# Attention rows and score maxima: other queues and routes for on-chip copies in a fused transformer block

## What is computed

```python
x = x + retention(layernorm(x))     # 4 heads, chunks along the tokens, gated
x = x + channel_mix(layernorm(x))   # sigmoid(xr @ W_r.T) * (relu(xk @ W_k.T)**2 @ W_v.T)
x = x + attention(layernorm(x))     # 16 heads of width 16, softmax with a bias by distance
x = x + channel_mix(layernorm(x))
```

## Time and profile before

| | us |
|---|---|
| median of 3 runs | 3273.11 (3270.3 to 3284.18) |
| the profiled execution | 3270.77 |
| its span, first to last instruction | 3268.8 |
| TensorE busy in it | 3028.9 |
| VectorE, ScalarE, GpSimd busy | 2026.8, 1731.7, 1249.1 |
| mean granted clock of TensorE | 0.949 of 2.4 GHz |

### The profile page before, as it was taken

The page is one execution under the profiler, slowest core; times in us unless marked ns, Lnnn a source line. Parts: engine busy times, 40 slices in busy tenths (PEclk is TensorE's granted clock), DMA queues, the critical chain, the costliest instruction groups (busy, mean ns, idle before and its releaser), DMA issues.

```text
span 3268.8 us, 50303 instructions
## 1 busy us (share of the span) xinstructions
PE 3028.9 (93%) x18786; PEld 1609.8 (49%) x18786; DVE 2026.8 (62%) x3231; ACT 1731.7 (53%) x3667; POOL 1249.1 (38%) x1764
## 2 busy tenths in 40 slices
PE   5969999899998999989999999999999999999998
PEld 3634456444564445644466444664446534465344
DVE  4448735687356863578545785458844588346882
ACT  2417844378343773438734486344754358533674
POOL 2314533245332452325433244333443334433353
PEclk8969999899998999989999899998999989999899
DMA  6060000600006000050001400023000320005100
GB/s 167 1 129 1 2 1 1 142 9 7 1 10 133 15 2 1 30 113 15 2 1 46 97 15 1 1 70 73 14 1 1 98 45 15 1 1 113 30 2 14
DMA packets 54897, 115.87 MB, mean 35 GB/s; under 512 B 10480, under 2 KB 33056, under 8 KB 54528
## 3 DMA queue, kind: packets, MB, share of 16 engines
q1 hardware_dynamic: 54656, 112.67, 15.5%
HBM read 69.24 MB, written 45.11 MB: 35 GB/s over the span
## 4 chain that ended last, share of the span: by engine, by line
PE 79%; DVE 7%; issue 3%; POOL 3%; DMA 3%; ACT 3%; SPq 1%; POOLq 0%; DVEq 0%; ACTq 0%
PE psum L647 18%; PE psum L701 18%; PE psum L523 11%; PE psum L678 9%; PE psum L752 3%; PE psum L546 3%; DMA SQ<-mrow 2%; PE psum L801 2%; PE psum L733 2%; PE psum L787 2%; PE psum L612 2%; PE psum L578 2%; DVE nrm L1238 2%; DVE mx L1358 2%; PE psum L804 2%
## 5 line engine op out<-in xcount | busy, mean ns | idle before, releaser
L1358 DVE TENSOR_REDUCE mx<-psum 128x1 f32<-128x1024 f32 x1024 | 1235.6, 1222 | 249.2 <-PE psum L647 247.1
L1108 ACT ACTIVATE Z<-psum 128x512 f32<-128x512 f32 x2048 | 1114.2, 597 | 411.5 <-PE psum L678 371.5
L1548 POOL TENSOR_TENSOR Z<-Z,band_exp 128x256 f32<-128x256 f32 (+1 forms) x1152 | 713.9, 641 | 932.0 <-ACT Z L1108 924.4
L678 PE MATMUL psum<-SQ,SK 64*128 64x512 f32 x2048 | 884.3, 481 | 39.8 <-DMA SQ<-mrow 39.8
L647 PE MATMUL psum<-SK,SQ 63*128 63x512 f32 x2048 | 798.0, 481 | 47.9 <-DVE mx L1358 27.6
L701 PE MATMUL psum<-Z,Vx 128*17 128x256 f32 x8192 | 643.5, 389 | 0.0
L647 PEld LDWEIGHTS psum<-SK,SQ 63*128 63x128 f32 x2048 | 330.8, 201 | 454.7 <-issue 292.7
L678 PEld LDWEIGHTS psum<-SQ,SK 64*128 64x128 f32 x2048 | 368.3, 189 | 236.7 <-ACT Z L1108 178.6
L523 PE MATMUL psum<-Wqkvg,Z 128*128 128x512 f32 x768 | 380.3, 620 | 18.5 <-ACT Z L1009 18.5
L701 PEld LDWEIGHTS psum<-Z,Vx 128*17 128x17 f32 x8192 | 138.5, 95 | 289.8 <-issue 272.5
L1493 POOL TENSOR_TENSOR Z<-Z 128x512 f32<-128x512 f32 x64 | 81.1, 1268 | 360.0 <-DVE Z L1286 353.9
(11 more groups left out here) (120 smaller groups left out, 3205.4 us busy)
## 6 DMA issues: line engine op xcount, KB each, us to landing
parts<-Z SPq DMA_DIRECT2D x48, 512.0 KB
SQ<-parts SPq DMA_DIRECT2D x48, 256.0 KB, 8.1
SK<-parts SPq DMA_DIRECT2D x48, 256.0 KB, 11.5
X<-L_attn_a_x SPq DMA_DIRECT2D x8, 1024.0 KB, 5.5
parts<-mixed SPq DMA_DIRECT2D x16, 512.0 KB
SQ<-parts SPq DMA_DIRECT2D x16, 512.0 KB, 8.3
SK<-parts SPq DMA_DIRECT2D x16, 512.0 KB, 13.8
out<-X SPq DMA_DIRECT2D x16, 512.0 KB, 8.0
```

The costliest lines, as they stand in the source:

```text
L678: pe.matmul(col_bank(s, i), SK[rows_of(h), h // 2, j * P:j * P + P], SQ[rows_of(h), h // 2, 512 * half:512 * half + 512], start=True, stop ...
L1108: nc.scalar.activation(ring[:, n % RING, :], col_bank(s, i), ACT.Exp)\
L1358: nc.vector.tensor_reduce(mx[:, blk, col:col + 1], bank_pair[u % 2], AX_X, ALU.max)\
L1548: nc.gpsimd.tensor_tensor(ring[:, n % RING, a:z], ring[:, n % RING, a:z], band_exp[:, 4 * hg + COLS[i], at:at + z - a], ALU.mult)\
```

## The change

For heads 0 to 3 the way through memory is replaced: 12 DMAs for q and 12 for k, each of 16 partitions by 1024 numbers, copy from `split[0][s]` to `SQ` or `SK` (`spread_directly`). The stores of heads 0 to 7 shrink to heads 4 to 7, and share 0 is gone. The semaphores are split in the same way: `first_out` (heads 4 to 7), `parts_out` (8 to 15), `spread_first` (the copies). The Relu of q = 2 waits for the copies and `first_out` of q. The maxima of block 0 are sent by ScalarE; SyncE sends those of blocks 1 to 7 and stores batch b−1 before them.

```diff
+        def max_rows_in(eng, blk):
+            h0, q0 = blk // 2 * 4, blk % 2 * 512
+            for hh in range(4):
+                r = HALF * (hh % 2) + MAX_ROW
+                eng.dma_start(SQ_words[r:r + 1, (h0 + hh) // 2, q0:q0 + 512],
+                              mrow[4 * hh:4 * hh + 4, blk % 2, :].bitcast(F32)).then_inc(mx_in[blk % 2].sem, 16)
...
+            def spread_directly(b, s):
+                need(sp, c_lo, b, 3 + s)
+                stack = (SQ_words, SK_words)[s]
+                for h in range(4):
+                    for group, part in enumerate(((1, 0, 0), (0, 1, 0))[s]):
+                        r0 = HALF * (h % 2) + HD * group
+                        sp.dma_start(stack[r0:r0 + HD, h // 2, :],
+                                     split[0][s][HD * h:HD * h + HD, part, :].bitcast(F32))\
+                            .then_inc(spread_first[s].sem, 16)
...
                 need(sp, c_lo, b, 4 * h + 3 + s)
+                p0 = (64, 0)[h]
+                done = (first_out, parts_out)[h][s]
                 for part in range(PARTS):
                     slot = (1 - part, part)[s]
-                    sp.dma_start(parts_scratch[s, 8 * h:8 * h + 8, slot],
-                                 split[h][s][:, part, :].bitcast(F32)).then_inc(parts_out[s].sem, 16)
+                    sp.dma_start(parts_scratch[s, (4, 8)[h]:8 * h + 8, slot],
+                                 split[h][s][p0:P, part, :].bitcast(F32)).then_inc(done.sem, 16)
...
             for b in range(B):
+                for s in range(2):
+                    spread_directly(b, s)
                 for h in range(2):
                     for s in range(2):
                         parts_store(b, h, s)
-                    for share in ((0, 1), (2,))[h]:
-                        for s in range(2):
-                            spread_rows(b, share, s)
-
-                for blk in range(8):
+                    for s in range(2):
+                        spread_rows(b, h + 1, s)
+
+                if b > 0:
+                    store(b - 1)
+                for blk in range(1, 8):
                     need(sp, mx_row, b, blk + 1)
...
                 if q == 2:
-                    need(act, parts_out[0], min(b + 1, B - 1), 2)
+                    need(act, spread_first[0], min(b + 1, B - 1), 12)
+                    need(act, first_out[0], min(b + 1, B - 1), 2)
...
                 max_rows(0)
-
-                for out_side in parts_out:
-                    need(act, out_side, b, 4)
+                need(act, mx_row, b, 1)
+                max_rows_in(act, 0)
+
+                for s in range(2):
+                    need(act, spread_first[s], b, 12)
+                    need(act, first_out[s], b, 2)
+                    need(act, parts_out[s], b, 2)
```

More of the change, by code:

```diff
@@ L265, in build @@
         c_lo = tally("dve", "c_lo", 8)
-        parts_out = [tally("sp", f"parts_out_{side}", 4, 16) for side in "qk"]
-        spread = [tally("sp", f"spread{share}", 8, 16) for share in range(3)]
+        first_out = [tally("sp", f"first_out_{side}", 2, 16) for side in "qk"]
+        parts_out = [tally("sp", f"parts_out_{side}", 2, 16) for side in "qk"]
+        spread_first = [tally("sp", f"spread_first_{side}", 12, 16) for side in "qk"]
+        spread = [None] + [tally("sp", f"spread{share}", 8, 16) for share in (1, 2)]
         p_vx = tally("pe", "p_vx", 4)
@@ L419, in _ @@
                 .then_inc(s_band, 16)
+            def spread_directly(b, s):
[7 more added lines that the diff above has]
+                            .then_inc(spread_first[s].sem, 16)
             def parts_store(b, h, s):
                 need(sp, c_lo, b, 4 * h + 3 + s)
+                p0 = (64, 0)[h]
+                done = (first_out, parts_out)[h][s]
                 for part in range(PARTS):
                     slot = (1 - part, part)[s]
-                    sp.dma_start(parts_scratch[s, 8 * h:8 * h + 8, slot],
-                                 split[h][s][:, part, :].bitcast(F32)).then_inc(parts_out[s].sem, 16)
+                    sp.dma_start(parts_scratch[s, (4, 8)[h]:8 * h + 8, slot],
+                                 split[h][s][p0:P, part, :].bitcast(F32)).then_inc(done.sem, 16)
             def spread_rows(b, share, s):
                 heads = SHARES[share]
-                need(sp, parts_out[s], b, 2 * (heads.start // 8) + 2)
+                need(sp, (first_out, parts_out)[share - 1][s], b, 2)
                 stack = (SQ_words, SK_words)[s]
@@ L452, in _ @@
                         parts_store(b, h, s)
-                    for share in ((0, 1), (2,))[h]:
-                        for s in range(2):
-                            spread_rows(b, share, s)
-                for blk in range(8):
-                    need(sp, mx_row, b, blk + 1)
[L459 to L465, removed]
+                    for s in range(2):
[3 more added lines that the diff above has]
+                for blk in range(1, 8):
+                    need(sp, mx_row, b, blk + 1)
+                    max_rows_in(sp, blk)
                     if blk == 4 and 0 < b < B - 1:
@@ L626, in rows_wait @@
             def rows_wait(b, u):
-                for share, heads in enumerate(SHARES):
-                    if u == NT * heads.start:
+                if u == 0:
+                    need(pe, spread_first[0], b, 12)
+                    need(pe, spread_first[1], b, 12)
+                for share in (1, 2):
+                    if u == NT * SHARES[share].start:
                         need(pe, spread[share], b, 8)
```

## The result

| | before | changed |
|---|---|---|
| median, us | 3273.24 (20 runs) | 3283.17 (20 runs) |
| ratio, with 95% interval | | 1.0024 (1.0016 to 1.0031) |
| the profiled execution, us | 3270.77 | 3276.07 |
| its span, us | 3268.8 | 3274.2 |
| TensorE busy, us | 3028.9 | 3034.6 |

What follows compares the result with a forecast made beforehand. TensorE, busy 93%, was taken as the bound, with at most 54 us of its waits recoverable. Terms +31 + 9 − 18 − 15 = +7 on 3270.8 gave 3278, as a median 3280 us; range 3238 to 3315.

Steps and rivals of the forecast that it cites:

- The copies: 24 copies of 64 KB at the head of SyncE's queue delay everything behind them by 15.1 us, bounds 13.0 to 16.0.
- the price by issue: Each of the 24 copies on SyncE costs 0.63 us to issue, 15.1 us together; the figure taken.
- The price by transfer: Moving the copies' 1.57 MB at 121 GB/s with the DMA engines full takes 13.0 us, the lower end.
- The half stores: The q stores of 4 heads, half the bytes, land no sooner than those of 8 heads did: 9.6 us.
- The Relu's wait: ScalarE's first Relu of mix 2 waits for copies and q stores, stalling TensorE: +31 us, plus 9 for a lower clock.
- R: Release of ScalarE's first Relu of mix 2, forecast 24.7 us after a batch's first store; free up to 20.7.
- The maxima: Block 0's maxima on ScalarE's queue land 4.7 us after issue, cutting TensorE's wait in batches 1 to 7: -18 us.
- rival (b): Another queue doesn't pass the transfers: block 0's maxima still land behind share 2; sum +60, 3333 us, chance 0.10.
- Batch 0: Earlier scores and maxima; the last stores of heads 8 to 15 end the wait at 227.6, not 242.86: -15 us.
- The sum: Whole kernel: +31 + 9 − 18 − 15 = +7 on the profiled 3270.8, so 3278; as a median 3280 us, +0.2%.

Runs made afterwards that it cites:

- the second run: The changed kernel with SyncE waiting for the maxima of block 0 before it stores batch b-1; 3280.9 us, 1.0023 of the kernel before.
- first run: The changed kernel with the q stores of heads 4 to 7 put between the q copies and the k copies; 3280.9 us, 1.0017 of before.
- the last run: The changed kernel with all copies ahead of the q stores, SyncE sending block 0's maxima, then share 2 and the output store; 3256.6 us, 0.9942 of before.
- the one-queue run: The changed kernel with q stores between the copies, SyncE sending block 0's maxima, then share 2 and the output store; 3214.2 us, 0.9818 of before.

## Why the prediction came true, step by step

The time (3280 forecast, 3283 measured) and the sign of the median are right. The terms are less so: two were off by 8 and 11 us in opposite directions, and that the total came so near is in part luck.

**The copies.** 15.1 us forecast, 15.1 measured: the price by issue held. The price by transfer, which took the engines as full at 98 to 121 GB/s, was not what bound them; they moved about as much with the engines only 0.60 busy. Two windows of the changed kernel (last three columns PEclk, DMA share, GB/s), the first with copies alone, the second with the 4-head stores:

```profile
966.00:968.00 2.00, 2.00 (x10) 1.71 (x9) 0.77 (x2) 0.70 (x2) 0.00 (x0) 1.00 0.60 98
980.00:982.00 2.00, 2.00 (x14) 1.80 (x13) 0.00 (x0) 0.00 (x0) 0.00 (x0) 1.00 0.26 107
```

**The half stores.** 9.6 us forecast, 8.7 measured (973.69 to 982.41), for half the bytes: 0.26 of the engines and 107 GB/s, against 0.51 and 209 for 8 heads. A quarter of 16 engines is 4, as "DMA: Bandwidth & Descriptors" of the Trainium skill, "Why a DMA increments its semaphore by 16 and not by 1", has it for a slowest dimension of 4.

**The Relu's wait.** The mechanism, its place and the batches are as forecast. With R at T+23.9 to T+24.6 `mix_kv` stood at T+26.7 to T+27.5 instead of T+23.6 to T+23.7: 3.0 to 3.8 us, 23 in seven batches, where I had 4.4 each, 31 together. In five of the seven batches it then took 5.2 to 5.4 us instead of 3.6 to 3.7, at a granted clock of 0.67 to 0.73 over these matmuls against 1.00 in the other two; from its start to the first score these five lost 1.5 to 1.8 us each, 8.5 in all, where I had 1.5 in six. Together 31.7, forecast 40. The term was 8 too large, all of it in the wait: R came up to 0.8 us earlier, and mix_kv started 2.8 to 3.1 us behind R, where I had 2.9 and 0.4 more for ScalarE.

**The maxima.** This step failed. I gave the landing 4.7 us and the gain 18; in batches 1 to 7 it took 5 to 8 us after the last issue and the gain was 7.1. The step was the argument against rival (b), that "a queue of its own has nothing ahead of these pieces": their queue had nothing ahead, but share 2 was still on the same engines, and they landed 0.9 to 1.9 us behind its end. The rule of the Trainium skill, "DMA: Bandwidth & Descriptors", "Issuing engines are not separate DMA queues", that several issuers save only issue time, described it better, and the trace agrees with it in these batches: on ScalarE's queue alone the waits were 40.9 us, on SyncE's 39.8. Rival (b) had its mechanism right in batches 1 to 7 and its landing near: T+70.9 forecast, T+67.8 to T+70.5 measured. What it charged on top for the output store (5 us a batch) the second run shows to be nothing, and in batch 0 it did not apply, since there the maxima went out ahead of share 2.

**Batch 0.** −15 forecast, −16.4 measured. Both terms of its last wait were close: the stores of heads 8 to 15 had landed by T+47.2 (forecast T+49.6), mrow at 225.9 (226.6). Since the stores came 2.4 us earlier than forecast, mrow and not they ended the wait. The run with the copies alone shows how the two parts depend on each other there: without the second queue the gain is lost, 23.1 us of wait.

**The sum.** 8 us too much on the Relu, 11 too much of a gain on the maxima, 1 too little in batch 0 and 3 unforeseen in the rest: 7 − 8 + 11 − 1 − 3 is the 5.4 measured, within rounding. The range held with room; the central value owes something to the two errors that cancel.

**What I did not see:** that the wait for the maxima was a matter of order. TensorE needs share 2 only at unit 64 (T+128 in the kernel before), some 60 us after the maxima land, and putting it behind them in the old queue is worth 1.7% (55 us between medians, 47 between profiles), about the 54 us that I gave as the most that the change could bring. The profile before had it: mrow landing late with the DMA engines full, beside a transfer that nobody was waiting for. The window from 1022 that I took for mrow's wait lies before mrow's issue at 1029.62; one inside the wait says the same, at another rate:

```profile
1032.00:1037.00 5.00, 2.90 (x5) 1.04 (x5) 3.19 (x3) 0.00 (x0) 0.00 (x0) 0.50 0.98 129
```

## What to carry to other kernels

Where a small transfer waits beside bulk ones, look at who waits for the bulk before looking for another queue; issue the small one ahead and hold the bulk back, which in one queue the order alone does. A second queue did not protect the small transfer here from a bulk one that was in flight or issued at the same moment; what it gave in batch 0 was an earlier issue. And before a queue gets more to issue, list what stands behind it: 15 us of cheap copies came out as a stall three engines away, because a store behind them freed a buffer.

## What the runs showed that I had not expected

- Four pieces of 2 KB on a queue of their own landed at most 1.1 us after the last issue with nothing else moving, and 8.4 us after it with 3 MB issued at the same time in the other queue. In one queue ahead of the same 3 MB TensorE ran on within 1.9 us. That the engines serve both queues in turn would fit; the runs show the times, not the turns.
- Removing the Relu's stall of 32 us alone (first run) brought some 2 us. Removing the wait for the maxima alone (the last run) brought some 27, and both together (the one-queue run) some 68. The Relu's stall costs next to nothing as long as share 2 sets the landing of the maxima, and its full price once it does not.
- TensorE waits 3.43 us at its first transposes of a batch, for GpSimd. The same wait is followed by a granted clock of 1.00 in some batches and of 0.50 (1.2 GHz) in others, in one and the same profile (the kernel before; the transposes, then the matmuls behind them, at the beginnings of batches 2 and 3):

```profile
845.67 0.66 PE L828 MATMUL psum<-ident,Z 128*128 128x128 f32 x4 [3.43 <-POOL Z L1500]
846.16 1.88 PE L523 MATMUL psum<-Wqkvg,Z 128*128 128x512 f32 x4
...
1244.50 1.12 PE L828 MATMUL psum<-ident,Z 128*128 128x128 f32 x4 [3.43 <-POOL Z L1500]
1245.41 3.62 PE L523 MATMUL psum<-Wqkvg,Z 128*128 128x512 f32 x4
```

The stretch from the first score by key to the next T is 331.9 us long in the first case and 334.7 in the second; that all of the 2.8 us comes from this place is not shown. With seven such stretches, two runs of one kernel, or two nearly equal kernels, can by this estimate differ by up to 20 us for nothing that the code says; the 20 runs of the kernel before lie 17 us apart (3267.2 to 3284.2). It is why a term of 5 us is better read in its own stretch than in the total.
